# Other engines and later places for the int32 weight casts of the first tile, in a linear-attention and gated-FFN layer

## What is computed

```python
q = elu(x @ Wq.T) + 1; k = elu(x @ Wk.T) + 1; v = x @ Wv.T      # 16 heads of 64
KV = einsum('bshd,bshe->bhde', k, v); z = q . k.sum(1)
x = layernorm(x + ((q @ KV) / (z + 1e-6)) @ Wo.T)
gate, up = x @ (w_gate/127).T, x @ (w_up/127).T                 # weights int32, 3072 x 1024
x = layernorm(x + (silu(gate) * up) @ (w_down/127).T)
```

## Time and profile before

| what | value |
|---|---|
| median of two runs | 1922.19 us |
| the two runs | 1917.21, 1927.16 us |
| the profiled execution, its own time | 1916.37 us |
| its span on the slowest core (core 1), first to last instruction | 1914.8 us |
| spans of the 8 cores | 1900.5 to 1914.8 us |
| mean granted TensorE clock of the cores | 0.938 to 0.944 of full speed |
| busy on core 1: PE, DVE, ACT, POOL | 1565.7, 597.0, 482.8, 37.6 us |

### The profile page before, as it was taken

How to read it: one execution, slowest core, us unless ns; L and a number is a source line. 1 busy time by engine, 2 the same in 40 slices (tenths; PEclk the granted TensorE clock), 3 DMA queues, 4 the chain that set the end, 5 groups by cost and what they waited for, 6 DMA issues and landing times.

```text
span 1914.8 us, 22987 instructions; the slowest of 8 cores (1900.5 to 1914.8 us)
## 1 busy us (share of the span) xinstructions
PE 1565.7 (82%) x7424; PEld 686.7 (36%) x7424; DVE 597.0 (31%) x1103; ACT 482.8 (25%) x681; POOL 37.6 (2%) x40
## 2 busy tenths in 40 slices
PE   0468763666799989989897888789899989989998
PEld 0123321222344434434343333334344434434443
DVE  0025243221352244235221333532352253135222
ACT  3343211211132214122212331231132223222212
POOL 0002000011000000000000000000000000000000
PEclk9879886899899999999998999999899999999999
DMA  4799526698335424422554442355245424522431
GB/s 144 192 265 305 147 89 181 183 255 254 100 100 154 138 67 121 154 78 56 188 153 121 83 100 94 89 142 152 64 107 156 128 72 132 151 70 67 127 111 44
DMA packets 213235, 255.28 MB, mean 133 GB/s; under 512 B 136320, under 2 KB 136320, under 8 KB 212096
## 3 DMA queue, kind: packets, MB, share of 16 engines
q1 hardware_dynamic: 213120, 253.81, 47.1%
HBM read 184.55 MB, written 37.75 MB: 116 GB/s over the span
## 4 chain that ended last, share of the span: by engine, by line
PE 66%; DMA 15%; DVE 8%; ACT 6%; issue 4%; SPq 1%; DVEq 0%; ACTq 0%
PE ps_c L713 17%; PE ps_a L1091 15%; PE ps_b L1104 15%; DMA outb<-wgi 6%; PE ps_b L915 5%; PE ps_a L530 3%; PE ps_b L530 3%; PE ps_a L544 2%; PE ps_b L544 2%; PE ps_a L793 2%; DVE t L805 2%; ACT texp L812 2%; DVE q_fm L819 2%; DMA res<-wq 1%; DMA res<-wo 1%
## 5 line engine op out<-in xcount | busy, mean ns | idle before, releaser
L1104 PE MATMUL ps_b<-ln1T,wgu 128*128 128x512 bf16 x1536 | 370.5, 385 | 37.8 <-DVE h_fm L1130 37.8
L1091 PE MATMUL ps_a<-ln1T,wgu 128*128 128x512 bf16 x1536 | 368.4, 383 | 26.7 <-ACT silu_b L1122 10.0
L713 PE MATMUL ps_c<-wd_buf,h_fm 128*128 128x512 bf16 x1536 | 352.2, 389 | 0.0
L1130 DVE SCALAR_TENSOR_TENSOR h_fm<-ps_b,silu_b 128x512 bf16<-128x512 f32 x192 | 131.9, 691 | 475.3 <-PE ps_b L1104 442.7
L1122 ACT ACTIVATE silu_b<-ps_a,consts 128x512 bf16<-128x512 f32 x192 | 131.1, 687 | 541.0 <-PE ps_a L1091 449.4
L1104 PEld LDWEIGHTS ps_b<-ln1T,wgu 128*128 128x128 bf16 x1536 | 150.6, 99 | 227.8 <-issue 54.0
L1091 PEld LDWEIGHTS ps_a<-ln1T,wgu 128*128 128x128 bf16 x1536 | 151.2, 99 | 215.3 <-issue 40.2
L713 PEld LDWEIGHTS ps_c<-wd_buf,h_fm 128*128 128x128 bf16 x1536 | 152.5, 100 | 184.4 <-issue 16.9
L793 PE MATMUL ps_a<-xT,wpair 128*128 128x512 bf16 x512 | 129.1, 404 | 31.3 <-DVE q_fm L819 26.5
L915 PE MATMUL ps_b<-wpair,attnT 128*128 128x512 bf16 x512 | 134.5, 423 | 22.9 <-DVE res L938 15.7
L530 PE MATMUL ps_a<-wpair,xT 128*128 128x512 bf16 x256 | 69.3, 432 | 100.4 <-DMA xT<-x_bf 82.6
(11 more groups left out here) (56 smaller groups left out, 834.9 us busy)
## 6 DMA issues: line engine op xcount, KB each, us to landing
wgu<-scr_wg SPq DMA_DIRECT2D x168, 256.0 KB, 2.7
wgu<-scr_wu SPq DMA_DIRECT2D x168, 256.0 KB, 2.8
x_f<-x SPq DMA_DIRECT2D x56, 512.0 KB, 4.3
out<-outb SPq DMA_DIRECT2D x32, 512.0 KB, 2.7
outb<-wgi SPq DMA_DIRECT2D x24, 512.0 KB, 5.3
outb<-wui SPq DMA_DIRECT2D x24, 512.0 KB, 5.1
outb<-wdi SPq DMA_DIRECT2D x12, 512.0 KB, 7.6
wgu<-wdi SPq DMA_DIRECT2D x12, 512.0 KB, 8.5
```

Of the source, the lines that this page charges most:

```text
L713: t.matmul(d_view[:, pr, hl * 512:(hl + 1) * 512], h_fm[:, hm, sc * 128:(sc + 1) * 128], wd_buf[:, hm, hl * 512:(hl + 1) * 512], start=(hm ...
L1091: t.matmul(ps_a[:, (m % 2) * 512:(m % 2 + 1) * 512], wgu[:, 0, r, j * 128:(j + 1) * 128], ln1T[:, j, :], start=(j == 0), stop=(j == NJ - 1)),
L1104: t.matmul(ps_b[:, (m % 2) * 512:(m % 2 + 1) * 512], wgu[:, 1, r, j * 128:(j + 1) * 128], ln1T[:, j, :], start=(j == 0), stop=(j == NJ - 1)),
L1130: v.scalar_tensor_tensor(h_fm[:, m, :], ps_b[:, (m % 2) * 512:(m % 2 + 1) * 512], INV127, silu_b[:, m % 2, :], ALU.mult, ALU.mult),
```

## The change

First, in the four fill jobs of the first phase 2 the gate casts are put on GpSimd too (`both_gp=True`), behind one another with the up casts. Second, in phase 3 of the first tile the gate cast stays on DVE, but it is written later: load_slab(m + 4) puts it on a list, and the next pass of the loop takes it from there first. The stores go with the casts, so their order on SP changes as well. No instruction is added and none is dropped.

```diff
-        def load_slab(m, first_tile=False):
+        def load_slab(m, first_tile=False, both_gp=False, defer_vec=None):
...
-                    ct = P.op("vector" if gi == 0 else "gpsimd",
-                              lambda e, gi=gi, r=r, sl=sl:
...
+                    def mk_ct(gi=gi, r=r, sl=sl, ld=ld, m=m, mat=mat,
+                              both_gp=both_gp):
+                        eng = "gpsimd" if (both_gp or gi == 1) else "vector"
+                        ct = P.op(eng,
+                                  lambda e, gi=gi, r=r, sl=sl:
+                                  e.tensor_copy(wgu[:, gi, r, :], stg_i32[sl]),
...
+                        slab_state["st"].append(mk_st)
+                        while len(slab_state["st"]) > 2:
+                            slab_state["st"].pop(0)()
+                    if gi == 0 and defer_vec is not None:
+                        defer_vec.append(mk_ct)
                     else:
...
+                        mk_ct()
...
+            vc = slab_state.setdefault("vc", [])
             for m in range(NM):
+                if vc:
+                    vc.pop(0)()
...
-                    load_slab(m + 4, first_tile)
+                    load_slab(m + 4, first_tile,
+                              defer_vec=(vc if first_tile else None))
...
-                    fj = [lambda m=m: load_slab(m, True) for m in range(4)]
+                    fj = [lambda m=m: load_slab(m, True, both_gp=True)
+                          for m in range(4)]
```

More of the change, by code:

```diff
@@ L1016, in load_slab @@
                     tr_outb[sl].end_write(ld)
-                    ct = P.op("vector" if gi == 0 else "gpsimd",
-                              lambda e, gi=gi, r=r, sl=sl:
[L1019 to L1027, removed]
-                    else:
[L1029 to L1037, removed]
@@ L1038, in load_slab, with mk_st @@
-                    w3_stores.append(mk_st)
-                    while len(w3_stores) > 2:
-                        w3_stores.pop(0)()
+                    def mk_ct(gi=gi, r=r, sl=sl, ld=ld, m=m, mat=mat,
[4 more added lines that the diff above has]
+                                  e.tensor_copy(wgu[:, gi, r, :], stg_i32[sl]),
+                                  waits=[ld, tr_wgu[gi][r].begin_write()]
+                                        + ([tr_stgi[2 + gi].begin_write()]
+                                           if m < 2 else []))
+                        tr_stgi[sl].add_reader(ct)
+                        tr_outb[sl].add_reader(ct)
+                        tr_wgu[gi][r].end_write(ct)
+                        if gi == 0:
+                            slab_state["lg"][m] = ct
+                        else:
+                            slab_state["lu"][m] = ct
+                        def mk_st(mat=mat, m=m, gi=gi, r=r, ct=ct):
+                            st = P.dma(f"scw{(2 * m + gi) % 2}",
+                                       lambda sy, mat=mat, m=m, gi=gi, r=r:
+                                       sy.dma_start(scr[mat][m], wgu[:, gi, r, :]),
+                                       waits=[ct], eng=BULKQ)
+                            tr_wgu[gi][r].add_reader(st)
+                            tr_scr[mat][m].add_write(st)
+                        slab_state["st"].append(mk_st)
+                        while len(slab_state["st"]) > 2:
+                            slab_state["st"].pop(0)()
@@ L1140, in phase3 @@
                     P.op("scalar", lambda e: e.preload_act_table(AF.Ln), waits=[t_si])
+            while vc:
+                vc.pop(0)()
             while w3_stores:
```

## The result

The changed kernel takes 0.9927 of the time before (95% interval 0.9903 to 0.9952): about 14 us less of 1918.9 (9 to 19), medians 1904.2 and 1918.9 us. That is less than 2%, as predicted, and the sign is clear of noise.

The account below looks back on a forecast made before the run. It took the first tile's int32 gate loads as the bound open to change (6% of span): latency in phase 2, DMA loads in phase 3. Terms -15.7 + 2.0 - 3.5 = -17.2 us gave 1902 us against 1919.2, range 1890 to 1919.

Parts of the forecast that it names:

- part 1: First phase 2, fill jobs' gate casts on POOL: PE's waits for DVE shrink, -15.7 us (bounds -3.5 and -24.3).
- at(1): Second attnT transpose on SP, first phase 2: issued at 299.5 us instead of 303.05, 3.5 us earlier.
- at(2): Third attnT transpose on SP, first phase 2: issued 10.0 us earlier, at 316.7, landing at most 4.9 us later.
- lt(0): First ln1T transpose on SP, first phase 2: issued at 302.9 us instead of 310.68.
- c2(3): PE's last c2 matmul group in the first phase 2: starts at 327.1 us instead of 342.80, as the preceding group ends.
- First step: Start of phase 3, first tile: the first gate cast, now behind h(0), starts later, +2.0 us.
- The 18 steps: Phase 3, first tile, after the first step: DMA bytes set each step, which stays 6.22 us; change 0.
- Tail: End of phase 3, first tile: two matmul groups fewer behind the last gate cast, -3.5 us (bounds 0 and -5.3).
- SP stays the bound: Rival for the first phase 2: only 3.5 us of the gain come through, -5.0 us in all, 1914.2; chance 0.18.
- More is gained: Rival: two PE matmul groups of phase 2 reach the upper clock, first step free, -23.4 us, 1895.8; chance 0.15.
- The stores bunch: Rival for phase 3: one more store ahead of each gate load, 1.04 us per step, +2.6 us, 1921.8; chance 0.08.
- Casts that meet: Rival for phase 3: DVE and POOL casts collide, 0.83 us more per step, -1.4 us in all, 1917.8; chance 0.07.

Follow-up runs that it names:

- e1: Kernel before with only the four fill jobs' gate casts moved to POOL, phase 3 as before; 0.9947 of the time before.
- e4: Changed kernel with the four fill slabs' loads and stores moved from SP to the GpSimd queue, loading already in phase 1; 0.9933 of before.
- e7: As e4, but the first fill load waits until Wq is read back at the end of phase 1; 0.9887 of before.
- e5: Changed kernel with phase 3's gate casts on POOL too, in the old place of the code; 0.9914 of before, 19 steps in 122.3 us.
- e0: Kernel before, run once more unchanged; no ratio given, its first tile's four stretches sum to 202.5 us against 203.0.
- e10: Changed kernel, run once more unchanged; 0.9937 of before.
- e6: Changed kernel with each gate slab of phase 3 of the first tile stored a second time; no ratio, 19 steps in 127.3 us against 116.5.
- e8: Changed kernel with two staging buffers per stream in phase 3 of the first tile; 0.9819 of before, 19 steps in 99.0 us.
- e3: Changed kernel with each store right behind its own stream's load in phase 3, as before; no ratio, 19 steps in 116.8 us.

## Why the prediction was right, and where it was not

The prediction was 1902 us and -17.2 us; measured were 1904.2 and -14 us, and -16.6 in the first tile alone. The kind of gain was right: part 1 takes a wait off PE, part 2 shortens the tail, and the steps stay. The sum came closer than its terms, and that is luck: part 1 gave 3.8 us less than predicted, and the three others together 3.2 more. By its steps, means over the cores:

- **Part 1**: -15.7 predicted, -11.9 measured (68.2 to 56.3), and e1 shows it alone. Along SP the times held, though partly because errors cancelled. Counted from at(0): at(1) was predicted at 12.35 us and came at 12.43 (300.60 - 288.17), gate load 3 at 25.85 and 25.79, at(2) at 29.55 and 29.18. Ahead of at(1) the first up load went out 0.8 us sooner than before, and POOL's cast of it took 0.8 us longer. lt(0) went out 1.5 us sooner than predicted (c2(0) started earlier and took 4.87 us), and its issue took 1.8 us longer than the 1.22 of before. Two steps behind it failed.
  - "at(2) lands at the latest 4.9 us later": it was 323.49 - 317.35 = 6.1 us. The landing maximum of before was no bound, since there at most one slab load was under way beside at(1) or at(2), and in the changed kernel two. For at(1) the cores show 2.7 to 2.9 us before, 5.7 to 6.8 after, 3.4 to 4.3 in e4, where all slab loads were done, and 5.2 to 9.8 in e7, where two were under way from POOL's queue: so what counts for at(1) is the loads beside it, not their place in SP's queue. It is not all: at(2) took 4.4 to 5.8 us in e4 and e7 with no slab load beside it, and 2.8 to 3.7 before with one; why stays open.
  - "c2(3) starts with c2(2)'s end": it waited 1.66 us for res, because all c2 share ps_b and DVE must have read it; before, the wait for the transpose hid that.
  - These two are 1.2 + 1.7 us, all of the difference on core 2 (68.73 - 55.85 = 12.9 of 15.7).
- **First step**: +2.0 predicted, +1.0 measured (5.69 to 6.65). Right in kind: the cast at 350.56 follows h(0), and e5, whose casts do not, has 5.7 us again.
- **The 18 steps**: 0 predicted; measured -1.6, and e0 and e10 lie 0.5 and 1.4 us from their twins, so it may be nothing. The value was right, its reason was not. "So the step is what the DMA engines carry" read 253 GB/s as a limit; e5, e6 and e8 show that it was the outcome of a loop through one staging buffer; that the bytes divided by that rate give the step is no test, since the rate was measured over those same steps. What spoke against it was there: a DMA share of 0.89 is not 1, another core had 0.79 in its steps, and each load went out 0.13 us behind the cast before it.
- **Tail**: -3.5 predicted, -4.1 measured (11.0 to 6.9).

Of the signs named, PE's two waits ahead of L839 were to be 1.5 to 4 us; they are 1.52 and 5.11, because the second has the layernorm in it. Phase 3 was to start near 340 us and starts at 344.02 on a core whose at(0) is 1.0 us later.

Of the rivals, *SP stays the bound* fell in its size, but its queue behind the slab loads is what was late next (e4, e7). *More is gained* fell: c2(0) took 4.87 us instead of 5.92, c2(2) no less than before. *The stores bunch* fell with e3. *Casts that meet* fell in phase 3: DVE's 20 casts stayed at 0.68 to 0.70 us on every core. None of the rivals said that the loop could be opened, and that was worth more than the change.

## What to carry to other kernels

A rate that is steady over many equal steps is not yet a limit: look whether each transfer waits for the consumer of the last, and if so, lengthen the consumer a little or give it a second buffer; the step answers at once. Moving a waiting instruction off an engine that has other work behind it helps until the next in-order queue that holds the same wait, here the DMA queue, so follow every queue that the waiting thing passes. Traffic moved to an earlier phase is free only where that phase leaves the DMA engines room.

## What the runs showed of the hardware

POOL and DVE met in the fill jobs. POOL's cast at 297.71 took 1.86 us instead of 1.04; it began while DVE squared res (L616), and a DVE instruction (L632) that takes 0.16 us at 332.31 took 0.54 at its end. Core 2 of the changed kernel, POOL and then DVE:

```profile
297.71 1.86 POOL L1023 CAST wgu<-outb 128x1024 bf16<-128x1024 int32 x1 [0.19 <-DMA outb<-wui]
```

```profile
297.44 1.23 DVE L616 SCALAR_TENSOR_TENSOR texp<-res 128x1024 bf16<-128x1024 f32 x1
...
299.04 0.54 DVE L632 SCALAR_TENSOR_TENSOR stats<-stats 128x1 f32<-128x1 f32 x1
```

POOL's cast ends at 299.57 and L632 at 299.58. L616 and L632 both read two SBUF operands. The Trainium skill (SBUF — State Buffer, Who interferes with whom) says that a VectorE instruction with two SBUF inputs contends with a GpSimd instruction that reads SBUF, that the port pair they share is an exclusive lock, and that issue order decides who blocks. These three rows agree in kind: each time the one that began second took longer. That POOL's cast waited for all of L616 they do not show, for it ended 0.90 us behind L616 and alone takes 1.04.

The issue of a transpose on SP, lt(0), took 3.01 us at 302.41, where 1.22 is usual; it came right behind at(1), with slab loads ahead of both. Over the cores lt(0) and lt(1) took 1.23 to 4.37 us to issue in the changed kernel and 1.22 to 1.23 in e7, where no slab load is on SP and neither follows another transpose so closely. Which of the two it is, and whether SP waits there for room in its queue, was not tried and stays open.
